# A recurrent gated block on one core: another order of the set-up, edge rows copied by VectorE, 18 squarings, one statistics operation fewer per chunk

## What is computed

```python
xn = ln(x)                                   # no gain, no bias
x_norm = ln(xn, ln_in_g, ln_in_b)            # a second norm, with gain and bias
x_norm = x_norm + conv3(x_norm) + conv_b     # depthwise, 3 taps over the tokens
gate, input_gate = split(x_norm @ gate_w.T + gate_b)
Bm = x_norm * sigmoid(input_gate) @ B_w.T + B_b
Cm = x_norm @ C_w.T + C_b
A_bar = expm(dt_A * A)                       # 64 x 64
for t in range(2048):                        # the recurrence, state of 64 per sequence
    s = ln(s @ A_bar + Bm[t], ln_st_g, ln_st_b)
    y[t] = Cm[t] * s
s = (y @ D_w.T + D_b) * sigmoid(gate)
g = silu(xn @ W.T + b + (xn @ V_r) @ C.T)
out = x + s * g
```

## Time and profile before

| | |
|---|---|
| runs | 2530.29, 2530.65, 2530.93 us; median 2530.65 |
| profiled execution | 2531.44 us, of which the span is 2529.6 us |
| busy in the span | PE 98%, DVE 87%, POOL 50%, ACT 40% |
| step 0 of chunk 0 starts (L871) | 81.41 us into the span |
| a chunk in the middle (234.31 to 310.33) | 76.02 us |
| last power of the recurrence starts | 2515.03 us |

### The profile page before, as it was taken

One profiled execution on the slowest core, in us unless ns is written; L12 is line 12 of the kernel. 1 busy time (PEld: TensorE's weight loads), 2 busy tenths in 40 slices (PEclk: granted clock), 3 DMA queues, 4 the chain that ended last, 5 costly groups with the idle time before them and its releaser, 6 DMA issues.

```text
span 2529.6 us, 42562 instructions
## 1 busy us (share of the span) xinstructions
PE 2478.2 (98%) x10057; PEld 1309.0 (52%) x10057; DVE 2200.3 (87%) x10947; ACT 1009.8 (40%) x1837; POOL 1271.0 (50%) x2465
## 2 busy tenths in 40 slices
PE   8899999999999999999999999999999999999996
PEld 5455555555555555555555555555555555555544
DVE  5788898888899888899888899888899888899887
ACT  3444344444334444334444334444334444334310
POOL 1355555455555455555455555455555455555443
PEclk9999999999999999999999999999999999999997
DMA  3112112122121122121122121221121221121121
GB/s 110 25 42 59 38 43 52 46 59 55 37 49 51 47 59 52 38 50 48 50 59 50 38 52 47 51 59 48 37 55 47 51 59 46 37 57 47 34 58 36
DMA packets 99606, 125.19 MB, mean 49 GB/s; under 512 B 31967, under 2 KB 48543, under 8 KB 99360
## 3 DMA queue, kind: packets, MB, share of 16 engines
q1 hardware_dynamic: 98624, 121.30, 19.5%
q10 hardware_dynamic: 736, 1.18, 0.2%
HBM read 71.96 MB, written 33.55 MB: 42 GB/s over the span
## 4 chain that ended last, share of the span: by engine, by line
POOL 49%; DVE 33%; issue 13%; PE 3%; POOLq 0%; DMA 0%; DVEq 0%; ACT 0%; ACTq 0%; SPq 0%
POOL dw L401 44%; DVE wq L860 14%; DVE dw L871 9%; DVE dw L885 9%; POOL ln L423 5%; PE bank L1116 1%; PE bank L1200 0%; PE bank L1195 0%; PE bank L1217 0%; POOLq L234 0%; POOL ln L425 0%; POOL ln L426 0%; POOL ln L427 0%; PE bank L1054 0%; POOL ln L440 0%
## 5 line engine op out<-in xcount | busy, mean ns | idle before, releaser
L401 POOL TENSOR_TENSOR dw<-q,minus_half 8x1 f32<-8x1 f32 x2048 | 1107.1, 541 | 1170.5 <-DVE wq L860 1140.0
L1180 PEld LDWEIGHTS bank<-Mscan,wT 128*65 128x65 f32 x2046 | 216.4, 136 | 654.5 <-issue 645.1
L1105 PE MATMUL bank<-xnorm,gateT 128*128 128x512 f32 x1024 | 506.4, 593 | 0.0
L860 DVE SCALAR_TENSOR_TENSOR wq<-dw 8x65 f32<-8x65 f32 x2048 | 443.2, 216 | 70.3
L1116 PE MATMUL bank<-xnorm,gateT 128*128 128x512 f32 x1024 | 501.8, 596 | 0.0
L1097 PE MATMUL bank<-xnT,WT 128*128 128x512 f32 x1024 | 494.0, 593 | 0.0
L1180 PE MATMUL bank<-Mscan,wT 128*65 128x128 f32 x2046 | 406.7, 280 | 25.3 <-DVE wT L888 15.3
L1181 PE MATMUL bank<-Mscan,wT 128*65 128x128 f32 x2046 | 391.7, 273 | 0.0
L885 DVE SCALAR_TENSOR_TENSOR dw<-dw 8x64 f32<-8x64 f32 x1024 | 280.0, 273 | 124.2 <-POOL dw L401 92.2
L871 DVE SCALAR_TENSOR_TENSOR dw<-dw 8x64 f32<-8x64 f32 x1024 | 280.6, 274 | 85.9 <-POOL dw L401 80.6
L875 DVE SCALAR_TENSOR_TENSOR dw<-bank,dw 8x128 f32<-8x128 f32 x1024 | 342.1, 334 | 1.9 <-PE bank L1181 1.6
(11 more groups left out here) (158 smaller groups left out, 2775.4 us busy)
## 6 DMA issues: line engine op xcount, KB each, us to landing
xc<-in_x SPq DMA_DIRECT2D x252, 128.0 KB, 2.8
xa<-in_x SPq DMA_DIRECT2D x252, 128.0 KB, 2.7
out<-o SPq DMA_DIRECT2D x248, 128.0 KB, 2.4
dw<-dtok SPq DMA_DIRECT2D x128, 96.0 KB
wtok<-dw SPq DMA_DIRECT2D x128, 33.0 KB
gateT<-in_gateT SPq DMA_DIRECT2D x1, 2048.0 KB
WT<-in_WT SPq DMA_DIRECT2D x1, 1024.0 KB, 8.0
xa<-in_x SPq DMA_DIRECT2D x4, 256.0 KB
```

The lines of the kernel that those rows point to most:

```text
L401: nc.gpsimd.tensor_tensor(dw[0:B, t, CR:CR + 1], q[:], minus_half[0:B, 0:1], ALU.pow).then_inc(s["r_ready"], 1)
L860: V.scalar_tensor_tensor(out=wq[:], in0=w_eps, scalar=1.0 / S, in1=w_eps, op0=ALU.mult, op1=ALU.mult, accum_out=q[:]).then_inc(s["q_ready" ...
L1105: ins = mm(mbank["gate", m][:], gateT[:, k, P * m:P * m + P], xnorm[p][:, k, :], start=(k == 0), stop=(k == KH - 1))
L1180: mm(scanP[0:WIDE, 0:2 * S], wT[:, 0:WIDE], Mscan[:, 0, :], start=True, stop=False)
```

## The change

It has five parts.

1. **Set-up, TensorE.** The 16 identity products are gone. The low-rank products of blocks 2 and 3 stand behind the two tiny products of the scaling. There are 18 squarings instead of 20, and the pieces of `PE_Z0`, `PE_IG0` and `PE_X0` stand at other squarings. After the last, three products stand ahead of the projection instead of five, the others behind `fill_d`.
2. **Set-up, VectorE and ScalarE.** The seven parameter operations stand behind rounds 9 to 12 of the series (`vec_ops`, `DVE_VEC`), with a semaphore of their own, `vec_ready`, for which ScalarE waits. The edge rows are copied out of the banks by VectorE (behind squarings 1 to 4), not by ScalarE. The low-rank sums stand at squarings 0, 1, 5 and 6. All statistics of chunk 2 and their aggregation stand at squarings 15 to 17.
3. **Recurrence.** In `odd_step` the wait for `d_in` stands ahead of the operation that raises `a_ready`, not behind it.
4. **POOL.** For chunks from 3 on the copy of the mean is gone: its readers take `sums` itself. So there are 12 operations, at t = 34 to 45, and ScalarE's next sums wait for all of them.
5. **First and last iteration.** In iteration 0 `fill_z` stands at t = 3, 3, 6, 6 and the taps at t = 7 to 22. In the last one, the first four gate pieces stand at t = 21, 24, 25, 26, and the first `gated_silu` at t = 29.

```diff
-SQUARINGS = 20
+SQUARINGS = 18
-POOL_LN = range(33, 46)
-
-PE_GATE_LAST = range(25, 41)
-V_G_LAST = (30, 31, 34, 37, 38, 41, 42, 45)
+POOL_LN = range(34, 46)
+PE_Z_FIRST = (3, 3, 6, 6)
+V_CONV_FIRST = range(7, 23)
+
+PE_GATE_LAST = (21, 24, 25, 26) + tuple(range(29, 41))
+V_G_LAST = (29, 30, 34, 37, 38, 41, 42, 45)
-PE_Z0 = (4, 6, 8, 10)
-DVE_WPRIME = (0, 1, 2, 3)
-DVE_CONV = (8, 10, 12, 14)
+PE_Z0 = (4, 5, 6, 7)
+DVE_WPRIME = (0, 1, 5, 6)
+DVE_HALO = (1, 2, 3, 4)
+DVE_CONV = (6, 8, 10, 12)
-PE_IG0 = (10, 11, 12, 12, 13, 14, 14, 15, 16, 16, 17, 18, 18, 19, 20, 20)
-PE_X0 = (17, 17, 19, 19)
-DVE_XG0 = (18, 19)
-DVE_STATS2 = (17, 18, 19)
+PE_IG0 = (8, 9, 9, 10, 10, 11, 12, 12, 13, 14, 14, 15, 15, 16, 16, 17)
+PE_X0 = (13, 13, 15, 15)
+DVE_XG0 = (16, 17)
+DVE_STATS2 = (15, 16, 17, 17)
+DVE_VEC = (8, 9, 10, 11)
...
                 else:
-                    m0, scale, var = sums[:, 0, :], (1.0, 1.0 / H), sums[:, 1, :]
+                    m0, scale, var = sums[:, 0, :], (None, 1.0 / H), sums[:, 1, :]
                 nm, a, r1, both, rr, bx, bz = (ln[:, a, :] for a in range(7))
+                if n >= 3:
+                    nm = m0
...
-                ] if n < 3 else first + [
+                ] if n < 3 else first[1:] + [
...
             def row_means(n):
                 wait_for(act, "xa_in", 16 * B, n, 0)
-                wait_ln(act, n - 1, 3)
+                wait_ln(act, n - 1, LN_OPS)
...
             act.wait_ge(s["consts"], 16 * 4)
-            act.wait_ge(s["dve_setup"], SETUP_VEC)
+            act.wait_ge(s["vec_ready"], VEC_OPS)
 
             normalise_z(0, xc, o)
             normalise_z(1)
-            for k in range(KH):
-                act.wait_ge(s["zfill"], k + 1)
-                a_(halo[:, k, :, 1:2 * NC + 1], hbank[k][:].rearrange("p (b m) -> p b m", b=B), ACT.Identity,
-                   bias=v_("ln_b", k), scale=v_("ln_g", k)).then_inc(s["y_done"], 1)
...
                 V.transpose(wT[0:32, 0:S], dw[:, t, CD:CM]).then_inc(s["wT_ready"], 1)
-                V.scalar_tensor_tensor(out=dw[0:B, t, CM:CM2], in0=dw[0:B, before, CM2:SLOT], scalar=r,
-                                       in1=dw[0:B, t, CM:CM2], op0=ALU.mult, op1=ALU.add).then_inc(s["a_ready"], 1)
                 if t % QT == QT - 1:
                     of, q = divmod(i * NQ + t // QT + 1, NQ)
                     if of < NC:
                         wait_for(dve, D_IN[q], 16, of, 16)
+                V.scalar_tensor_tensor(out=dw[0:B, t, CM:CM2], in0=dw[0:B, before, CM2:SLOT], scalar=r,
+                                       in1=dw[0:B, t, CM:CM2], op0=ALU.mult, op1=ALU.add).then_inc(s["a_ready"], 1)
...
+            def vec_op(k):
+                wait_for(dve, "vec_ready", 1, k, 0)
+                vec_ops[k]().then_inc(s["vec_ready"], 1)
...
+                for k in range(VEC_OPS):
+                    if DVE_VEC[k // 2] == TERMS - n:
+                        vec_op(k)
...
+                if n in DVE_HALO:
+                    k = DVE_HALO.index(n)
+                    if k == 0:
+                        dve.wait_ge(s["halo_zeroed"], KH)
+                    dve.wait_ge(s["zfill"], k + 1)
+                    V.tensor_scalar(halo[:, k, :, 1:2 * NC + 1], hbank[k][:].rearrange("p (b m) -> p b m", b=B),
+                                    v_("ln_g", k), v_("ln_b", k), ALU.mult, ALU.add).then_inc(s["y_done"], 1)
...
-            for k in range(KH):
+            def low_rank(k):
                 mm(wbank[k][:], VT[:, P * k:P * k + P], CrT[:], start=True, stop=True).then_inc(s["wprime_mm"], 1)
+
+            for k in range(2):
+                low_rank(k)
             pe.wait_ge(s["consts"], 16 * 4)
-
-            def keep_busy(n):
-                for _ in range(n):
-                    mm(banks[7][:, 0:P], ident[:], ident[:], start=True, stop=True)
-
-            keep_busy(4)
...
+            for k in range(2, KH):
+                low_rank(k)
...
-LN_OPS = 13
-LN_Z = 8
+LN_OPS = 12
+LN_Z = 7
```

More of the change, by code:

```diff
@@ L625, in _ @@
             input_gate(0, 3)
[L626 removed]
+            act.wait_ge(s["dve_setup"], SETUP_M + 2)
             copy_dT(0)
@@ L966, in _ @@
                         right_tap(0, DVE_CONV.index(n - 1), h, 0)
-                if n in DVE_STATS2:
-                    bn_stats(2, DVE_STATS2.index(n), 0)
-                    bn_stats(2, DVE_STATS2.index(n), 1)
+                for j in range(NJ):
+                    if DVE_STATS2[j] == n:
+                        for h in range(2):
+                            bn_stats(2, j, h)
+                if n == DVE_STATS2[-1]:
+                    aggregate(2)
                 if n in DVE_XG0:
@@ L992, in _ @@
             dve.wait_ge(s["pe_setup"], SQ_END + 3)
+            link(V.tensor_copy(vT[:], scanP[0:S, 2 * S:2 * S + B]))
+            dve.wait_ge(s["pool_cleared"], 3)
+            link(V.tensor_copy(dw[0:B, CT - 1, CM:CM2], scanP[0:B, 3 * S:4 * S]))
             link(V.tensor_copy(Mscan[0:32, :, :], scanP[0:32, 4 * S:8 * S].rearrange("p (h e) -> p h e", h=2)))
             assert done[0] == SETUP_END
-            for h in range(2):
-                bn_stats(2, NJ - 1, h)
-            aggregate(2)
             def iteration(i, p, parts):
@@ L1005, in iteration @@
                     if A:
-                        if t in V_CONV:
-                            k, part = divmod(V_CONV.index(t), 4)
+                        if t in conv_at:
+                            k, part = divmod(conv_at.index(t), 4)
                             if part < 2:
@@ L1250, in _ @@
                 b_proj(0, k, -1, False)
-            pe.wait_ge(s["dve_setup"], SETUP_M + 5)
-            mm(scanP[0:B, 0:2 * S], vT[:], Dcat[0:S, S:], start=True, stop=True).then_inc(s["p_ready"], 1)
+            pe.wait_ge(s["dve_setup"], SETUP_M + 3)
+            for q in range(NQ):
+                fill_d(0, q, -1, False)
+            mm(scanP[0:S, 2 * S:2 * S + B], AC[:], st_b_wide[:, 0:B], start=True, stop=True)
+            mm(scanP[0:B, 3 * S:4 * S], st_b_wide[:, 0:B], AC[:], start=True, stop=True)
             for h in range(2):
@@ L1256, in _ @@
             ins.then_inc(s["pe_setup"], 1)
-            for q in range(NQ):
-                fill_d(0, q, -1, False)
+            pe.wait_ge(s["dve_setup"], SETUP_END)
+            mm(scanP[0:B, 0:2 * S], vT[:], Dcat[0:S, S:], start=True, stop=True).then_inc(s["p_ready"], 1)
             pe.wait_ge(s["dve_setup"], SETUP_END)
@@ L1315, in _ @@
             last_fill_o(3)
-LN_OPS = 13
-LN_Z = 8
+LN_OPS = 12
+LN_Z = 7
 SETUP_LN = 7
 SETUP_LN_Z = 5
-SETUP_VEC = 7
-SETUP_SERIES = SETUP_VEC + 11
+VEC_OPS = 7
+SETUP_SERIES = 11
 SETUP_M = SETUP_SERIES + TERMS + 1 + SQUARINGS + 4
```

49 lines of the change are left out of this document (22 added, 27 removed).

## The result

Median 2510.8 us (4 runs, 2510.45 to 2511.14) against 2530.79 us of the kernel before on the same chip: ratio 0.9921, 95% interval 0.9904 to 0.9938, 20.0 us faster. The forecast was 2525.05, its range ended at 2522.0. The profiled execution has a span of 2508.5 us (before 2529.6).

The account below looks back on a forecast made before the run. The recurrence between POOL and VectorE was taken to set the time. Savings of 3.5 (wait), 1.7 (set-up) and 0.4 (first iteration), 5.6 in all, took the profiled 2531.44 to 2525.84, 2525.05 us on the median's scale; range 2522.0 to 2528.8.

Parts of the forecast that it names:

- POOL: one operation fewer: POOL's row in the recurrence: removing L425 at t = 33 is worth 0, at the other end -1.5 us.
- The third wait: Recurrence, t = 31 and 63: moving VectorE's wait off the path saves 0.055 at 64 sites, -3.5 us.
- The set-up, -1.7: Ahead of the recurrence: step 0 starts at 79.7 instead of 81.41, -1.7 us; ends +0.5 and -4.
- gains nothing: Rival on the set-up: its early gain is lost to ScalarE, low-rank sum and VectorE's tail; 2526.8 us, chance 0.17.
- Opening, series, edge rows and squarings: Set-up stages: series from 11.45 to 23.1, edge rows ready at 26.4, squaring 17 at 63.0 us.
- two tiny products fewer and no wait give 0.6, `dT` starts at 72.4: End of set-up, TensorE's projection: 0.6 us saved there, `dT` at 72.4 instead of 74.09.
- First iteration, -0.4: Chunk 0, step 2: VectorE's 0.53 wait for a look-ahead product goes as `fill_z` comes later, -0.4 us.
- Last iteration, 0: Last iteration: gate pieces move within a stretch without long steps, 0, within one piece (0.86 us) either way.
- the first steps of POOL's row: Rival: a long step of POOL's operations also goes, or set-up stands are shorter; about -1.5 more, 2523.5 us, chance 0.18.
- the moved wait: Rival in the recurrence: the wait still costs on L894 and then on `a_ready`; 2528.6 us, chance 0.10.
- the clock did not stay low through the gate: Rival denied here: TensorE's clock stays low through the input gate, 0.98 more per piece, up to 2538.6 us, chance 0.03.
- chunks of 75.9 us: Sign that the forecast is right: each chunk of the recurrence takes 75.9 us, where it took 76.0.

Follow-up runs that it names:

- POOL's part alone: Kernel before with only the copy of the mean removed from chunks 3 on, 12 operations at t = 34 to 45: 2512.91 us for 2531.81.
- the copy put back: Changed kernel with POOL's copy of the mean restored, 13 operations at t = 33 to 45: 2529.11 us for 2531.81.
- the set-up alone: Changed kernel with recurrence, POOL's row, first and last iteration as in the kernel before: 2532.16 us for 2531.81.
- the statistics in the middle: Changed kernel with the set-up's last statistics moved to VectorE's stand behind the copy of Dcat, no identity products: 2509.64 us for 2530.36.
- them last: Changed kernel with z's last two statistics and their aggregation back behind VectorE's end of the set-up: 2510.98 us for 2529.26.
- the run with ten probes: Changed kernel with ten extra POOL operations, at t = 10 in chunks 2 to 18 and t = 50 in chunk 20: 2511.41 us.

## Why the prediction was wrong

**POOL: one operation fewer, "I take 0", other end -1.5: this step failed.** It was worth 17 to 19 us (18.9 alone; 17.3 worked out as 2014 powers at 8.6 ns, from 538.7 to 530.1 in traces whose first 33 powers are alike; in the two profiles of before and after the difference is 10.6, of which 1.8 are there in the first 33 powers already). I read L425's own step and found it no longer than its neighbour; but that neighbour was already long. I had the starts of all 2048 powers and looked for steps longer than their median, 1.184, whereas the first 31 steps of chunk 0 took 1.175. The untested assumption was that an operation costs only where it stands. The rule of the Trainium skill that I weighed there ("SBUF — State Buffer", two engines blocking each other at the shared port pair) looked at the same place: L886 still takes 0.31 beside L432, and what was gained lies in the powers. Whether that rule has a part in the powers' own length, no run shows.

**The third wait, -3.5: held.** The long steps t = 31 and 63 are gone, and the most frequent chunk is 0.10 shorter than with POOL's part alone (75.26 for 75.36; the means of chunks 1 to 30, 75.33 and 75.41, differ by 0.07). Between the copy put back and the set-up alone, both with long powers, it is 0.11 in the mean. By itself the wait measured -2.1, interval -0.2 to -5.1.

**The set-up, -1.7: failed at its end, and so the rival "gains nothing" (0.17) held for this part.** Opening, series, edge rows and squarings came within 0.7 us of the forecast, with VectorE's copies at 0.81 instead of 0.6, hidden as said. The step that fell is "two tiny products fewer and no wait give 0.6, `dT` starts at 72.4": I counted the eight products at the higher clock, and in the stand of 2.85 us ahead of them the clock had fallen. `dT` came 2.0 late, step 0 only 1.35, since it followed 6.6 us behind `dT` and not 7.3: from the first issue of D's transfer to step 0 it took 4.28 instead of 4.92. For the clock I asked only when it rises (46.1 forecast, 45.4 in the trace), not whether it falls again. The page "TensorE: Matmul & The Clock Gate" of the Trainium skill, in its closing table, asks for a TensorE that is kept fed, and I had weighed that against the series alone. At the end of the set-up the trace agrees with it: with 21 identity products there the clock stayed up, and from the last squaring's copy to `dT` it took 8.01 us instead of 9.08 with the statistics in the middle, and 8.00 instead of 10.71 with them last. The clock column of the earlier trace rows reads 1.00 although I called the level low there; the trace has no record of the clock ahead of 50.4, and what shows the level is the same squaring's 0.47 us in the earlier trace rows and 0.33 in the earlier trace rows.

**First iteration, -0.4:** worth 0.2 by the traces (0.66 for 0.47). **Last iteration, 0:** not tried by itself. In the traces the last chunk takes 74.8 to 76.5 us, 75.4 in the mean, with the old order (7 kernels), and 74.6 to 77.8, 76.2 in the mean, with the new one (13 kernels): no gain, and if anything a loss.

**The sum:** 17.3 for POOL, 3.5 for the wait, 0.4 of the set-up and 0.2 of the first iteration make 21.4; the clock's fall in chunk 0 took 1.1 in the profiled execution. 20.3 stand against the measured 20.0. Part of that agreement is luck: the sum leaves out the 1.8 ns that the first 33 powers already differ by, up to 3.6 us, and takes the wait at its full 3.5 and the set-up from one execution. Read directly from the starts of the powers in the two profiles, the first power is 0.4 us earlier, chunk 0 is 0.5 longer, chunks 1 to 30 together are 21.3 shorter, and what follows is the same; these profiles do not divide the 21.3 between powers, level and wait.

Of the other rivals, none happened: the first steps of POOL's row stayed long (1.21 and 1.22), the moved wait does not cost, and the clock did not stay low through the gate. The price of this last one doesn't follow from its terms: the forecast has 14 pieces at the higher level, and 14 x 0.98 is 13.7, not 13.5 from 15. Of my signs, "chunks of 75.9 us" told at once that the recurrence was misjudged: they took 75.3.

## What to carry to other kernels

Take the instruction that sets the rhythm of a long loop and compare its duration ahead of and behind the first occurrence of everything else on its engine: eight nanoseconds in two thousand steps were worth more here than all the reordering of the set-up. Before a stand is shortened, ask on every engine what else ends there; here POOL's statistics, TensorE's clock and the transfer each took some of the gain. Price the products behind a stand at both levels of the clock, and look at more than one profile before calling a microsecond of a set-up won.

## What was not expected of the hardware

POOL's power of a loop that alternates with VectorE ran at 527 and 533 ns in turn (530 and 534 in other executions), or at 538 to 540 in every step; once long, it stayed so for the rest of the run. A single operation of 0.22 us with one constant behind an odd step's power (t = 33 or 51) tipped it into the second; the same at t = 10, 34 or 50, or the form with two constants (0.18 us) at t = 33, did not, and nothing tried ended it. (At t = 10 the powers were not in the usual alternation when it was tried.) Following the longer of the two powers isn't enough: in the run with ten probes the even steps had become the longer ones (535), and t = 10 of chunk 6 tipped nothing. Whether an odd step is enough while the even ones are longer is open. Odd and even steps differ in what VectorE does meanwhile (L886 and L889, or L872 and L876). What in POOL or between the two holds this state stays open, and so does what sets the levels 530.1 and 531.9 from one execution to the next, and when both steps take 527.6.
